# A new order of the attention rounds, folded weights, and the shared expert's first loads inside the last rounds

## What is computed

```
frames = windows of 100 samples, every 160; power spectrum (51 bins)
h  = (log(power @ mel.T + 1e-6) @ dct.T) @ w_proj + b_proj        # 40 mels, 13 coefficients
x  = layernorm(h)
# attention, 8 heads: keys of 64, values of 24
h1 = rmsnorm(x) * norm1_w;  q, k, v = h1 @ wq, h1 @ wk, h1 @ wv
scores = (q k^T + (q w_pos) basis + u k + (v w_pos) basis) / 8    # basis: 32 relative positions
x  = softmax(scores) v @ wo + bo + x
x  = x + gelu(rmsnorm(x) * norm2_w @ w1 + b1) @ w2 + b2
h  = h + x
# mixture of experts on layernorm(h)
each of 16 experts takes the 1000 tokens of the highest sigmoid score,
  y[token] += score * (silu(x Wg) * (x Wu)) Wd                    # width 768
h  = h + y + (silu(x Ws_g) * (x Ws_u)) Ws_d                       # shared expert, width 384
```

## Time and profile before

| | us |
|---|---|
| median of 3 runs | 2250.64 (2248.63 to 2255.05) |
| the profiled execution | 2256.45 |
| its span, first to last instruction | 2254.7 |
| attention part, first product to last store issued | 30 to 1238 |
| granted TensorE clock, mean | 0.98 |

### The profile page before, as it was taken

How to read it: one execution, slowest core, us unless ns; L and a number is a source line. 1 busy time by engine, 2 the same in 40 slices (tenths; PEclk the granted TensorE clock), 3 DMA queues, 4 the chain that set the end, 5 groups by cost and what they waited for, 6 DMA issues and landing times. The chain is left out here.

```text
span 2254.7 us, 46810 instructions
## 1 busy us (share of the span) xinstructions
PE 2069.0 (92%) x13522; PEld 1700.7 (75%) x13522; DVE 1365.8 (61%) x3632; ACT 1103.7 (49%) x2680; POOL 704.0 (31%) x587
## 2 busy tenths in 40 slices
PE   2999999999999999999996699989999999999997
PEld 1677777777777777777774577778888888888886
DVE  1577767677776767677673577744555554555531
ACT  2677777767777777777763222122222222222221
POOL 0122122121212212121221000236665566665563
PEclk9899999999999999999997899999999999999998
DMA  5555655555555655555561633325454444454442
GB/s 142 156 146 147 168 143 163 148 158 151 151 163 144 167 147 155 150 156 161 143 165 50 161 103 102 93 54 89 91 97 77 73 78 88 91 98 76 73 80 31
DMA packets 317544, 272.43 MB, mean 121 GB/s; under 512 B 80740, under 2 KB 304822, under 8 KB 317494
## 3 DMA queue, kind: packets, MB, share of 16 engines
q1 hardware_dynamic: 238374, 235.01, 39.0%
q0 software_dynamic: 70656, 30.65, 9.6%
q10 hardware_dynamic: 8464, 6.15, 0.9%
HBM read 150.73 MB, written 120.54 MB: 120 GB/s over the span
## 5 line engine op out<-in xcount | busy, mean ns | idle before, releaser
L1134 POOL DMA_INDIRECT out<-ff_y,ff_idxs x128 | 261.8, 2045 | 245.5 <-DVE ff_y L1417 187.9
L1194 ACT ACTIVATE ff_sg<-ffp_g 128x500 f32<-128x500 f32 x192 | 112.9, 588 | 400.3 <-PE ffp_g L1529 369.9
L1121 POOL DMA_INDIRECT ff_xg<-xs_d,ff_idxg x128 | 205.1, 1603 | 297.1 <-issue 283.6
L468 ACT ACTIVATE sb_prob<-sb_ssb,sb_mx 125x250 f32<-125x250 f32 x512 | 253.1, 501 | 58.6 <-DVE sb_mx L562 58.6
L1541 PE MATMUL ffp_d<-ff_wd,ff_wide 128*125 128x192 f32 x1536 | 261.2, 327 | 16.0 <-DVE ff_wide L1404 15.2
L1404 DVE TENSOR_TENSOR ff_wide<-ff_sg,ffp_u 128x500 f32<-128x500 f32 x192 | 129.4, 674 | 221.1 <-PE ffp_u L1529 219.5
L1541 PEld LDWEIGHTS ffp_d<-ff_wd,ff_wide 128*125 128x125 f32 x1536 | 247.8, 188 | 19.9 <-issue 18.2
L1529 PE MATMUL ffp_g<-ff_xsp,ff_wsp 128*128 128x500 f32 x960 | 251.8, 392 | 1.6 <-DVE ff_xsp L1276 1.6
L1529 PE MATMUL ffp_u<-ff_xsp,ff_wsp 128*128 128x500 f32 x960 | 249.6, 390 | 0.0
L548 DVE COPY sb_ptsb<-ps_ptps 125x500 f32<-125x500 f32 x256 | 172.9, 675 | 123.8 <-PE ps_ptps L716 120.6
L1529 PEld LDWEIGHTS ffp_g<-ff_xsp,ff_wsp 128*128 128x128 f32 x960 | 180.2, 189 | 39.3 <-issue 2.7
(11 more groups left out here) (181 smaller groups left out, 3664.4 us busy)
## 6 DMA issues: line engine op xcount, KB each, us to landing
bias_d<-sb_rsb SPq DMA_DIRECT2D x256, 219.6 KB
sb_bsk<-bias_d SPq DMA_DIRECT2D x256, 218.8 KB
hx_d<-sb_hx SPq DMA_DIRECT2D x32, 336.0 KB
sb_hxl<-hx_d SPq DMA_DIRECT2D x32, 336.0 KB
ff_wd<-WdT SPq DMA_DIRECT2D x16, 576.0 KB
xs_d<-sb_xs SPq DMA_DIRECT2D x32, 238.0 KB
bias_d<-sb_rsb SPq DMA_DIRECT2D x256, 25.5 KB
sb_bsk<-bias_d SPq DMA_DIRECT2D x256, 25.4 KB
```

The costliest lines, as they stand in the source:

```text
L468: a.activation(prob[:, s % 2, t], ssb[:, s % 2, t], ACT.Exp, bias=mx[:, s % 2, t:t + 1], scale=-1.0, accum_out=rs[:, t, s:s + 1]).then_inc ...
L1121: g.indirect_dma_start(xg[:, t], None, xs_d[:, :], bass.IndirectOffsetOnAxis(idxg[:, t:t + 1], 0), bounds_check=last).then_inc(gat, 16)
L1134: g.indirect_dma_start(out_d[:, :], bass.IndirectOffsetOnAxis(idxs[:, t:t + 1], 0), y[:, t], None, bounds_check=last, compute_op=ALU.add). ...
```

## The change

1. *Order.* In each engine's `body` the steps of a round are put in another order: on TensorE `qk(0)`, values and the transposes for `xnT` now stand before the row inverses in slot 0; on VectorE `h1` and its statistics go from slot 6 to 7 and stand before `pt_copy`, `xnT` from slot 0 to slot 1 behind `qw` and `pt_copy`, `x1` to slot 3, the tokenizer's statistics to slot 4; the V copies go from ScalarE to VectorE; `xb` on GpSimd waits until `h2n` is done; the score transposes use another bank and slot 3. The load of the exponential table goes behind the `rsb` copies of the next slot.
2. *Folded weights.* `dct` and `w_proj` are multiplied once at the start (`wmel`, 41 rows with the bias), and `wq` with `w_pos` (`folded`), so that `qw` comes from `hsp` by five split matmuls for two pairs of heads (slots 1 and 5).
3. *Values* of four heads in one call; row inverses by `transpose`; all three parts of `w1` in one go, the third in another bank.
4. *Shared expert.* `load_shared`, `shared_high` and `shared_low` stand at the head of the last rounds; chunk 0 of the second part no longer loads and splits.

The diff, cut to its core. The uses of the banks:

```diff
-        T_USES, C_USES, D_USES, Q_USES = 5, 5, 3, 18
+        T_USES, C_USES, D_USES, Q_USES = 4, 5, 3, 16
-        QW_USE = [1, 5, 11, 15]
+        QW_USE = [1, 10]
+        QW_SLOT = {1: 0, 5: 1}
```

SP:

```diff
+            def load_shared():
+                for i, src in enumerate((w["WsgT"], w["WsuT"])):
+                    sp.dma_start(sh.wraw[:, i, 0], src[0:128]).then_inc(sh.ld, 16)
+                    for half in range(2):
+                        sp.dma_start(sh.wraw[half * 64:half * 64 + 64, i, 1], src[128:D]).then_inc(sh.ld, 16)
+                for dst, src in ((sh.wd[:], w["WsdT"].rearrange("(k p) n -> p k n", p=128)), (sh.blocks[:], w["blocks"])):
+                    sp.dma_start(dst, src).then_inc(sh.ld, 16)
+                sp.wait_ge(c_st, 80 * (CHUNK // FRAMES))
+                sp.dma_start(sh.xraw[:, 0, 0], xnT_d[0:128, 0:CHUNK]).then_inc(sh.x_ld[0], 16)
...
             def body(bt, bq, bb_, bc, bd):
+                if bb_ is None and bc is not None:
+                    load_shared()
```

ScalarE and VectorE (`shared_low` is the same for the low parts):

```diff
+            def shared_high():
+                act.wait_ge(sh.ld, 16 * 8)
+                for i in range(2):
+                    a.activation(sh.wsp[:, i, 0], sh.wraw[:, i, 0], ACT.Copy).then_inc(sh.w_hi, 1)
+                    a.activation(sh.wsp[:, i, 2], sh.wraw[:, i, 1], ACT.Copy).then_inc(sh.w_hi, 1)
...
+                if bc is None and bd is not None:
+                    shared_high()
                 for s in range(SLOTS):
+                    if bt is not None and s == 4 or bc is not None and s == 6:
+                        tables_stale = True
...
+                    if tables_stale:
+                        a.preload_act_table_set(EXP_SET)
...
+                    if bq is not None and s in QW_SLOT:
+                        use = QW_USE[QW_SLOT[s]]
+                        done = 4 * bq + 2 * QW_SLOT[s]
+                        halves = slice(0, 64), slice(64, 128)
+                        dve.wait_ge(q_mm, Q_USES * bq + use + 1)
+                        for i in range(2):
+                            p = 2 * QW_SLOT[s] + i
+                            v.tensor_scalar(qw[halves[i], i], qps[use % 2][halves[i], 0:FRAMES], cq[halves[i], p:p + 1], None, ALU.add).then_inc(qw_hi, 1)
+                        for i in range(2):
+                            p = 2 * QW_SLOT[s] + i
+                            dve.wait_ge(qw_hi, done + i + 1)
+                            v.scalar_tensor_tensor(out=qw[halves[1 - i], i], in0=qps[use % 2][halves[i], 0:FRAMES], scalar=cq[halves[i], p:p + 1],
+                                                   in1=qw[halves[i], i].bitcast(F32), op0=ALU.add, op1=ALU.subtract).then_inc(q_ev[use % 2], 1)
```

TensorE:

```diff
             for p in range(PAIRS):
+                for k in range(2):
+                    for i in range(2):
+                        rows = slice(64 * i, 64 * i + 64)
+                        m(folded(i, k)[:, p], wqT[rows, p, k * 128:(k + 1) * 128], wpz[rows, p, 0, i], start=True, stop=True)
+            m(qps[1][0:MELS, 0:D], dct[:], wproj[:], start=True, stop=True)
...
-                            ins = m(tps[:, k * FRAMES + t * TP:k * FRAMES + (t + 1) * TP], each, ident[0:TP, 0:TP], start=True, stop=True)
+                            ins = nc.tensor.transpose(tps[:, k * FRAMES + t * TP:k * FRAMES + (t + 1) * TP], each, ident[0:TP, 0:TP])
...
+            def quad_values(b, k):
...
+                    pe.wait_ge(pt_ev, HEADS * b + QUAD * (k + 1))
                     for j in range(NT):
-                        for i in range(2):
+                        for i in range(QUAD):
+                            ins = m(otps[VC * i:VC * i + VC, k], vz[:, j, QUAD * k + i], ptsb[:, i, j], start=j == 0, stop=j == NT - 1)
...
+                    if bq is not None and s in QW_SLOT:
+                        use = QW_USE[QW_SLOT[s]]
+                        q_freed(pe, bq, use)
+                        col = ALL_COLS + 128 * QW_SLOT[s]
+                        for k, (wk, xp, xk) in enumerate(PARTS):
+                            ins = m(qps[use % 2][:, 0:FRAMES], wsp[:, wk, col:col + 128], hsp[:, xp, xk], start=k == 0, stop=k == len(PARTS) - 1)
+                        ins.then_inc(q_mm, 1)
```

Second part, SP:

```diff
-            for i, src in enumerate((w["WsgT"], w["WsuT"])):
-                sp.dma_start(s_wraw[:, i, 0], src[0:128]).then_inc(s_ld, 16)
...
+                if not isinstance(c, int) or c > 0:
+                    wait(sp, x_lo, 2 * (c - 1))
+                    sp.dma_start(s_xraw[:, par, 0], xnT_d[0:128, own]).then_inc(x_ld[par], 16)
```

More of the change, by code:

```diff
@@ L386, in _ @@
             g.memset(braw[:], 0.0).then_inc(z_set, 1)
[L387 removed]
+            g.memset(logmel[:], 1.0).then_inc(z_set, 1)
             g.memset(vz[:], 0.0).then_inc(z_set, 1)
@@ L568, in body @@
                         pt_copy(bb_, s - 1)
+                    if bq is not None and s == 3:
+                        for t in range(NT):
+                            dve.wait_ge(q_mm, Q_USES * bq + V_USE[t] + 1)
+                            if t == 0:
+                                wait(dve, vz_in, 2 * bq)
+                            v.tensor_copy(vtmp[:, t], qps[V_USE[t] % 2][0:TP, 0:D]).then_inc(q_ev[V_USE[t] % 2], 2)
+                    if bd is not None and s == 1:
+                        dve.wait_ge(d_mm, D_USES * bd + 1)
+                        wait(dve, c_st, 80 * bd)
+                        v.tensor_copy(xnT[:], bank2(cps, FRAMES, KD)).then_inc(d_ev, 1)
                     if bc is not None and s == 1:
@@ L667, in body @@
                         ins.then_inc(t_ev, 1)
+                    if bc is not None and s == 7:
+                        b0 = D_CHAIN * bc
+                        dve.wait_ge(d_ch, b0 + 6)
+                        for t in range(NT):
+                            v.tensor_scalar(xs[:, t, 0:D], h1[:, t], c_mv[:, t, 0:1], d_y[:, t:t + 1], ALU.subtract, ALU.mult).then_inc(d_ch, 1)
             rounds(dve, body)
@@ L792, in body @@
-                    if bc is not None and s == 5:
-                        pe.wait_ge(c_ev, C_USES * bc + 2)
-                        ps = bank2(cps, FRAMES, 128)
-                        for j in range(2):
-                            col = COLS["w1"][0] + j * 128
-                            for k, (wk, xp, xk) in enumerate(PARTS):
-                                ins = m(ps[:, j], wsp[:, wk, col:col + 128], h2sp[:, xp, xk], start=k == 0, stop=k == len(PARTS) - 1)
-                        ins.then_inc(c_mm, 1)
@@ new lines, in body @@
+                    if bq is not None and s == 4:
+                        qk(bq, 2)
+                    if bc is not None and s == 4:
+                        if bd is not None:
+                            pe.wait_ge(d_ev, D_USES * bd + 3)
+                        pe.wait_ge(c_ch, C_CHAIN * bc + C_CHAIN)
+                        pe.wait_ge(c_ev, C_USES * bc + 1)
+                        transposes(bank2(cps, FRAMES, 128), h2n, c_mm)
+                    if s == 4:
+                        quad_values(bb_, 0)
@@ new lines, in body @@
+                    if bc is not None and s == 5:
+                        pe.wait_ge(c_ev, C_USES * bc + 2)
+                        ps = bank2(cps, FRAMES, 128)
+                        for j in range(DFF // 128):
+                            col = COLS["w1"][0] + j * 128
+                            if j == 2 and bt is not None:
+                                pe.wait_ge(t_ev, T_USES * bt + 3)
+                            for k, (wk, xp, xk) in enumerate(PARTS):
+                                ins = m(ps[:, j] if j < 2 else tps[:, 0:FRAMES], wsp[:, wk, col:col + 128], h2sp[:, xp, xk], start=k == 0, stop=k == len(PARTS) - 1)
+                            if j > 0:
+                                ins.then_inc(c_mm, 1)
```

449 lines of the change are left out of this document (211 added, 238 removed).

## The result

The changed kernel takes **2277.9 us** (median of 4 runs, 2276.9 to 2279.1), the kernel before 2252.9 beside it (4 runs). The ratio is 1.0113, 95% interval 1.0093 to 1.0133: **slower by 25 us**, where 2221 was predicted and the range ended at 2253. What came is the rival of 8%, *the clock falls in the wait for xnT*, priced at 2269.

What follows compares the result with a forecast made beforehand. The prediction took TensorE to bound the attention part, with most of its saved work going into waits. Its terms, -13 - 3 - 5 - 8.5 = -29.5 us, gave 2221 us at the median's level; stated range 2160 to 2253.

Steps and rivals of the forecast that it cites:

- the clock falls in the wait for xnT: Rival, 8%: the idle before the gate matmuls halves TensorE's clock, adding some 1.7 us a round; 2269, slower.
- the third: Slot 1: VectorE splits qw and does copy 0 before xnT, so the gate matmuls wait and TensorE idles 2.2 us.
- idle before gate, w1, values, qk(3): TensorE waits each round for xnT, h2sp, probability copy 7 and a bank: 2.2, 1.0, 0.85 and 0.6 us.
- call of sixteen: Values of four heads side by side on TensorE: 0.97 us a call, with 1.94 as the other bound.
- steady rounds: 28 full attention rounds, each 35.5 us, a gain of 0.47 a round: -13 us (-44 to +10).
- first rounds: Start of the attention part: folding adds +4.5, shorter early rounds give -1.7 and -5.8; together -3 us (-7 to +4).
- last rounds, without the splits: Three rounds without new batches: earlier third gelu block, halved row inverses, no xb delay; -5 us (-9 to +2).
- join and splits: Shared weights loaded before the second part: -11.1 at its start, +2.6 for splits ahead of xnT; -8.5 us (-11 to -4).
- the walk along the waits: One round followed in six steps from w2 to w2 across engines: period 35.0 to 35.7, taken as 35.5 us.
- The order holds and TensorE's work decides: Rival, 12%: waits in the round stay at the 2 us of before; period 32.5, kernel 2137.
- Values in fours run as pairs: Rival, 10%: the values call on TensorE costs 1.0 more, period 36.5; 2249, no change.
- ScalarE loads tables more often: Rival, 2%: rsb copies behind log or gelu force two more table loads of 1.28; period 38.1, 2294, slower.

Runs made afterwards that it cites:

- experiment 1: The changed kernel with VectorE copying xnT before it splits qw, as the kernel before did: 2137.4 us, ratio 0.9465, a round 32.67.
- experiment 2: The changed kernel, wait for xnT left, its idle filled with two sets of unneeded score-sized matmuls on TensorE: 2224.8 us, ratio 0.9854, a round 35.31.
- experiment 5: The changed kernel, wait for xnT left; h2sp's low part moved ahead of short statistics instructions, probability copy 7 and reciprocal ahead of head 0's scores: 2281.2 us, ratio 1.0108.
- experiment 6: The kernel before, with VectorE's xnT copy moved behind probability copy 0 and an extra spare copy ahead of that: 2393.2 us, ratio 1.060, a round 40.43.
- experiment 3: The kernel before, old round order, with only the shared expert's loads and splits moved into the attention part's last rounds: 2249.8 us, ratio 0.9965.
- experiment 7: The changed kernel with one set of unneeded score-sized matmuls (1.04 us) in its wait for xnT: 2258.0 us, ratio 1.002, 9 runs.
- experiment 8: The changed kernel with xnT copied first, value matmuls inside a call reordered to heads 0 and 1, then 2 and 3: 2139.1 us, ratio 0.9483.
- experiment 9: The changed kernel with xnT copied first, each values call parted into two of two heads, h2n or xs transposes between: 2151.3 us, ratio 0.9553.

## Why the prediction was wrong

**The step that failed is the third**: "2.2 us idle" was priced at its own length. The wait was there, 2.37, at the place and for the reason given. What it did to the clock stood apart, as a rival with 8%, at 1.7 us a round; it measured 2.2. Experiments 1, 2, 5 and 6 show it from four sides: no wait, no fall; the wait but no idle, no fall; the other waits gone, the fall stays; the old work with such a wait, the fall comes.

The row that spoke for it was in the prediction: TensorE busy 4.25 of 8.70 us with waits up to 2.15, and then 0.65. I read it as the effect of a thin stretch, with half the time idle, and took 63% busy for safe. Experiment 6 refutes that reading: there TensorE is full on both sides of one idle of 1.94. The Trainium skill, "TensorE: Matmul & The Clock Gate", section A second HAM failure mode: psum-queue depth-cycling, says of another kernel that small idles between groups of matmuls, if they come often, make the clock swing. The traces agree in part: small idles did it (falls with 1.33, 1.94 and 2.37 us), but one of them a round was enough, and the three shorter ones a round that experiment 1 leaves (1.13, 0.52, 0.28) did nothing. The table in the section Why this matters for your kernels, on the same page of the Trainium skill, is laxer on single gaps and would have let idles of all three lengths pass; here the measurement decides against it.

The other terms, against what was measured:

| term of the sum | predicted | measured |
|---|---|---|
| round at full clock | 35.5 | 35.31 (experiment 2) |
| TensorE's own work in it | 30.3 to 30.5 | 30.67 (32.67 less 2.00 of idle, experiment 1) |
| idle before gate, w1, values, qk(3) | 2.2, 1.0, 0.85, 0.6 | 2.37, 1.14, 0.52, 0.28 |
| call of sixteen | 0.97 | 0.98 |
| VectorE and ScalarE a round | 25.6 and 25.8 | 25.3 and 25.5 |
| steady rounds, in all | -13 (28 rounds) | +41.0 (27 rounds): -17.6 without the falls, by experiment 2, and +58.6 by them |
| first rounds | -3 | -5.6 (the first `dft` came 3.1 later, +4.5 was taken) |
| last rounds, without the splits | -5 | -3.2 (to the end of the last `xs`) |
| join and splits | -8.5 | -7.9 (experiment 3); -11.8 in this trace (from the last `xs` on) |

Without the falls the last four lines add up to -34 to -38, and the span of experiment 2 is 31.3 shorter than that of the kernel before; the predicted sum was -29.5. So the walk along the waits was right to 0.2 us in 35, and the error is one term, 2.2 us a round, that was set at zero. That it came so near is in part luck: the walk gave five waits 4.95 us, and four measure 4.31 while the fifth, 0.3 before qk(0), isn't there; TensorE's own work and idles too short to be marked made up for it. The last rounds' term can't be told from scatter: from the last `dft` to the end of `xs` the kernel before took 121.0 us and the kernel of experiment 3, with the same instructions up to there but for the shared expert's loads and copies, 118.2. The second part from the table's load on took 995.9 to 1004.5 in the eleven kernels with the new join, for no reason that I found, and 1010.0 and 1010.2 in the two with the old one; the -13.8 of the changed kernel is at the good end of that.

*The rivals.* "The order holds and TensorE's work decides" gave a round of 32.5 and 2137. The changed kernel is far from it, but one moved copy leads there (32.67, 2137). "Values in fours run as pairs" is refuted by the rows of L807. "ScalarE loads tables more often" too: in ten rounds (400 to 775 us) the groups of ScalarE show four loads a round, as before, and the `rsb` copies behind log and gelu add none.

```profile
L511 ACT ACT_TABLE_LOAD x20 | 25.7, 1283 | 0.4
...
L536 ACT ACT_TABLE_LOAD x10 | 12.8, 1283 | 0.2
L549 ACT ACT_TABLE_LOAD x10 | 12.8, 1283 | 0.2
```

## What to carry to other kernels

Where TensorE bounds a stretch at full clock, an idle on it can have two prices: its length, and the matrix work behind it that then runs at 1.2 GHz. Here the second was nearly as large as the first (2.2 and 2.6 us), and it made a change that took work away slower than no change. After lightening the bounding engine, look for its longest single wait first, and ask of the engine that releases it whether it stood idle itself just before: here a copy of 0.67 us stood in line behind an instruction that was waiting for something else, and moving it took the ratio from 1.011 to 0.947. If a wait can't be removed, filling it with matmuls that nobody needs is a fair test of what the clock costs, and here was a gain of 2.6% by itself.

## What the runs showed of the hardware

**How short an idle can cost the clock.** With 2.37 us of idle the clock fell in every round (the changed kernel, experiment 5), with 1.94 in 22 of 26 (experiment 6), with 1.33 in 17 of 26 (experiment 7); with 1.13 and 0.52, the longest left in experiment 1, it never did in 26 steady rounds. In these traces the fall starts between 0.7 us before the end of the idle and 2.6 us behind it. With one and the same idle, rounds of the same instructions differ, and so do runs of one kernel (20 us apart in experiment 7).

**Column strips take their instructions separately.** In experiment 8 the first eight instructions of a call belong to two strips of the array, the next eight to the two others. In the trace the third and fourth matmul still start 26 and 33 ns behind the first, and the next four 0.2 us later. The profile doesn't name the strips, but it marks the instructions that raise the semaphore, one for each head: two of them stand among the first eight, and all four start last of the sixteen, within 33 ns. So the strips that stood further back in the text started before waiting instructions in front of them. Order inside a call made no difference there; other work between the calls (experiment 9) did part them.

**Four strips at no extra time.** 16 matmuls of 125 x 250 in 32 columns each took 0.98 us, 8 of them in two strips 0.97. The Trainium skill, "TensorE: Matmul & The Clock Gate", section Part 3, has 2.38 times for three column tiles; here four run at twice the rate of two.
